# Graph network on one core: adjacency cast by GpSimd's loads, one bf16 copy of its rows read for two heads, operand halves made beside the first masks, flag read inside the last loop, output in four pieces

## What is computed

```python
# layer 0: attention over the neighbours, 4 heads of 64
ht = (h @ Wm).reshape(n, 4, 64); el = ht.al; er = ht.ar
scores = leaky_relu(el[:, :, None] + er.T[None], 0.2), -inf where adj == 0
out = softmax(scores) @ ht
# layer 1: GRU cell on (adj without diagonal) @ h; attention with 3 heads of 256,
# whose weights depend on the column alone; a second GRU cell on the mean of the heads
att = softmax(where(adj > 0, e[None, :], NEG_INF)); support += (att * adj) @ (h @ W)
# layer 2: concat(h, adj @ h / (deg + 1)) @ W.T
# layer 3: adds a term only where an adjacency value lies strictly between 0 and 1
```

## Time and profile before

| | |
|---|---|
| median of 3 runs | 1352.21 us |
| the profiled execution | 1358.34 us |
| its span | 1356.5 us, mean granted clock 0.929 |
| PE busy | 1152.5 us, 85% |
| DVE busy | 974.1 us, 72% |
| ACT busy | 808.2 us, 60% |
| POOL busy | 322.9 us, 24% |
| moved by DMA | 225.10 MB |
| a half row (704 KB), issue to landing, median | 5.3 us |

### The profile page before, as it was taken

The page is one execution under the profiler, slowest core; times in us unless marked ns, Lnnn a source line. Parts: engine busy times, 40 slices in busy tenths (PEclk is TensorE's granted clock), DMA queues, the critical chain, the costliest instruction groups (busy, mean ns, idle before and its releaser), DMA issues.

```text
span 1356.5 us, 35957 instructions
## 1 busy us (share of the span) xinstructions
PE 1152.5 (85%) x15055; PEld 944.2 (70%) x15055; DVE 974.1 (72%) x2219; ACT 808.2 (60%) x1232; POOL 322.9 (24%) x383
## 2 busy tenths in 40 slices
PE   4519888999867999899867999999899997778996
PEld 3419888999856776566635888887788654436885
DVE  5599897899983576676776999897995364552541
ACT  3468898999752233322326999897889365653000
POOL 4762323133041032333232111111120142220000
PEclk9859999999875999989987999999899998899998
DMA  9733445111026667677779778677752010020532
GB/s 320 241 135 121 176 131 186 35 35 66 3 71 214 198 222 253 211 246 254 272 257 345 228 273 323 220 249 250 263 191 102 5 32 13 18 92 1 192 108 84
DMA packets 89450, 225.10 MB, mean 166 GB/s; under 512 B 7506, under 2 KB 52674, under 8 KB 89026
## 3 DMA queue, kind: packets, MB, share of 16 engines
q1 hardware_dynamic: 88097, 222.21, 48.5%
q10 hardware_dynamic: 1184, 0.53, 0.1%
HBM read 202.98 MB, written 19.73 MB: 164 GB/s over the span
## 4 chain that ended last, share of the span: by engine, by line
PE 49%; DVE 16%; DMA 15%; issue 6%; ACT 6%; POOL 5%; SPq 1%; DVEq 0%; ACTq 0%; POOLq 0%
PE PS L1676 12%; DMA arena<-in_adj 12%; PE PS L1817 10%; PE PS L1818 10%; PE PS L1871 8%; DVE scratch L1372 3%; PE PS L1767 3%; DVE arena L1214 2%; PE PS L1858 2%; DVE arena L1220 2%; DVE arena L1160 2%; PE PS L1774 1%; PE PS L1711 1%; POOL X L738 1%; ACT arena L823 1%
## 5 line engine op out<-in xcount | busy, mean ns | idle before, releaser
L1817 PE MATMUL PS<-arena 128*128 128x257 f16 x1452 | 331.6, 276 | 21.5 <-ACT arena L968 14.9
L1818 PE MATMUL PS<-arena 128*128 128x257 f16 x1452 | 331.4, 277 | 0.0
L1676 PE MATMUL PS<-arena 128*128 128x65 f16 x7744 | 260.9, 196 | 72.3 <-DVE arena L1220 56.9
L1676 PEld LDWEIGHTS PS<-arena 128*128 128x128 fp8e4 x7744 | 257.3, 99 | 75.8 <-issue 59.9
L1372 DVE CUSTOM_DVE_ANT_0 scratch<-arena 128x1408 bf16<-128x1408 f32 x132 | 216.4, 1639 | 78.7 <-DMA arena<-in_adj 46.1
L865 ACT ACTIVATE arena<-arena 128x1024 fp8e4<-128x1024 f32 (+1 forms) x231 | 227.6, 1079 | 21.1 <-DVE arena L1214 20.7
L968 ACT ACTIVATE arena<-arena 128x896 int16<-128x896 uint8 (+1 forms) x198 | 187.3, 971 | 31.9 <-DVE arena L1425 22.4
L1817 PEld LDWEIGHTS PS<-arena 128*128 128x128 bf16 x1452 | 144.3, 99 | 47.5 <-ACT arena L968 13.2
L1818 PEld LDWEIGHTS PS<-arena 128*128 128x128 bf16 x1452 | 141.6, 97 | 23.1
L959 ACT ACTIVATE arena<-arena,E1B 128x896 uint8<-128x896 f32 (+1 forms) x131 | 139.1, 1062 | 13.1 <-DMA arena<-m_rows 13.1
L1214 DVE TENSOR_TENSOR arena<-arena,AT 128x256 int32<-128x256 int32 (+1 forms) x264 | 115.4, 437 | 26.7 <-ACT arena L865 23.8
(11 more groups left out here) (187 smaller groups left out, 1537.6 us busy)
## 6 DMA issues: line engine op xcount, KB each, us to landing
arena<-in_adj SPq DMA_DIRECT2D x176, 704.0 KB, 5.3
arena<-in_adjT SPq DMA_DIRECT2D x44, 512.0 KB, 7.6
hw_saved<-arena SPq DMA_DIRECT2D x22, 387.0 KB, 7.3
arena<-in_adjT SPq DMA_DIRECT2D x22, 384.0 KB, 5.1
arena<-hw_saved SPq DMA_DIRECT2D x9, 774.0 KB, 7.8
arena<-h_saved SPq DMA_DIRECT2D x44, 128.0 KB, 2.1
arena<-e_rows SPq DMA_DIRECT2D x3, 1408.0 KB, 7.3
arena<-el_rows SPq DMA_DIRECT2D x8, 512.0 KB, 5.4
```

The source lines that it names most:

```text
L1676: ins = pe.matmul(PS[:, k, q * C0:(q + 1) * C0], MASK[:, (m + j) % NMASK, q, k * P:(k + 1) * P], MOV[:, j, 2 * h + q, a, :], start=(j == 0 ...
L1817: pe.matmul(PS[:, k, 0:D + 1], weights, w[:, 0:D + 1], start=(j == 0), stop=False)
L1818: ins = pe.matmul(PS[:, k, 0:D + 1], weights, w[:, D + 2:2 * D + 3], start=False, stop=(j == NT - 1))
```

## The change

1. `STG`, `load_chunk`, `casts_at` and POOL's 66 casts go. POOL issues DMAs that read fp32 and write fp8 straight into `AT`: 22 of 128x768 (group A) ahead of all six splits, and 22 of 128x2048 (B and C) when all of `MOV` is there. The first mask of a group waits for all 22 transfers. SP does not load blocks any more; its first task after x is the six weight pieces.
2. Behind them POOL issues 22 DMAs from HBM to HBM that make a bf16 copy of the adjacency's rows (`AH_D`). Diagonal blocks, loaded by SP as fp32, are cleared by one POOL operation (128x2816) and written over the copy by 22 small DMAs. SP waits for all 44 before its loads of the edge weights.
3. The maxima read the bf16 copy, in a ring of two buffers. Each half row is loaded once for heads 0 and 1 (`EB` now holds both heads' scores): 88 maxima in steps 0 to 19 of the GRU stage, and 44 for head 2 in the attention, from step 8 on, one every 2.25 steps. `clear_diagonal` goes. The maxima of heads 0 and 1 are turned, saved and loaded together; those of head 2 are turned at step 19 of unit 4 and step 0 of unit 5.
4. The `MOV` loop is cut up: DVE does `weighted(m + 2)` and `low_part(m)` ahead of the masks of step m of unit 0, ACT `weighted_high(j + 2)` ahead of its threshold.
5. The flag is made after block 20 of the last loop, and the output is written in four pieces (8, 7, 5 and 2 blocks) and the remainder.

```diff
@@ the preamble @@
-            for n in range(4):
-                load_chunk(n)
             for i in range(4):
                 load_piece(RAW[:, i, :], pieces[i], f"raw{i}")
...
+            for i in range(len(pieces)):
+                sp.wait_ge(sem("ws"), i + 1)
+                save_piece(HALF[:, i % 4, :, :], pieces[i], f"ws_out{i % 4}")
+                if i + 4 < len(pieces):
+                    load_piece(RAW[:, i % 4, :], pieces[i + 4], f"raw{i % 4}")
             sp.wait_ge(sem("el_t"), 1)
             sp.dma_start(EL_D.rearrange("t h q -> (t h) q"), ELT[0:NT * H0, :]).then_inc(sem("el_rows"), 16)
             sp.wait_ge(sem("el_rows"), 16)
             load_el(0)
             load_el(1)
...
-            sp.wait_ge(sem("stg_used"), len(chunk0) - NT)
+            sp.wait_ge(sem("rows_h"), 16 * 2 * NT)
@@ POOL @@
             for t in range(NT):
-                pool.wait_ge(sem(f"stg{t % 4}"), 16 * (t // 4 + 1))
-                pool.tensor_copy(AT[:, t, 0:GA[0][1] * P], STG[:, t % 4, 0:GA[0][1] * P], saturate=False
-                                 ).then_inc(sem("stg_cast"), 1)
...
+                pool.dma_start(AT[:, t, 0:GA[0][1] * P], adjT[t, :, 0:GA[0][1] * P]).then_inc(sem("adj_a"), 16)
+            for i in range(len(pieces)):
+                pool.wait_ge(sem(f"raw{i % 4}"), 16 * (i // 4 + 1))
...
+                split(RAW[:, i % 4, :], HALF[:, i % 4, :, :], pieces[i][3], 3 * D)
...
             pool.wait_ge(sem("mov"), NT)
...
+            for t in range(NT):
+                pool.dma_start(AT[:, t, GA[0][1] * P:NT * P], adjT[t, :, GA[0][1] * P:NT * P]).then_inc(sem("adj_b"), 16)
+            for t in range(NT):
+                pool.dma_start(AH_D[t], t_in["adj"][t * P:(t + 1) * P, :]).then_inc(sem("rows_h"), 16)
+            pool.wait_ge(sem("dblk"), 16 * NT)
+            link(pool.tensor_tensor(DBLK, DBLK, NOTI[:].unsqueeze(1).to_broadcast([P, NT, P]), ALU.mult))
+            pool.wait_ge(sem("rows_h"), 16 * NT)
+            for t in range(NT):
+                pool.dma_start(AH_D[t, :, t * P:(t + 1) * P], DBLK[:, t, :]).then_inc(sem("rows_h"), 16)
@@ DVE, masks of layer 0 @@
-                if h == 0:
-                    dve.wait_ge(sem("stg_cast" if g == 0 else "stg_used"), j + 1 + (g - 1) * NT if g else j + 1)
+                if h == 0 and j == 0:
+                    dve.wait_ge(sem("adj_a" if g == 0 else "adj_b"), 16 * NT)
...
+            weighted(0)
+            weighted(1)
             for m in range(last + 1):
                 n, j = divmod(m, NT)
+                if m + 2 < NT:
+                    weighted(m + 2)
+                if m < NT:
+                    low_part(m)
                 positive_mask(m)
@@ maxima @@
+        PAIRED = 2 * 2 * NT
+            return min(PAIRED, -(-PAIRED * t // ROWS_LAST))
+        row_at = {8 + 9 * i // 4: 2 * NT + i for i in range(2 * NT)}
...
             def load_row(L):
...
+                if L >= 2:
+                    sp.wait_ge(sem("rmax"), maxima_after(L - 2))
+                sp.dma_start(AROW[:, L % 2, :], AH_D[t, :, c * QUARTER:(c + 1) * QUARTER]
+                             ).then_inc(sem(f"arow{L % 2}"), 16)
...
-            load_scores(EB, 0)
+            load_scores(EB[:, 0, :], 0)
+            load_scores(EB[:, 1, :], 1)
...
-                if (n, j) == (1, 18):
-                    maxima_turned(1, PS[0:NT, 7, 0:P])
-                if (n, j) == (5, 13):
-                    maxima_turned(2, PS[0:NT, 7, 0:P])
+                if (n, j) == (5, 0):
+                    maxima_turned(2, 1, 7)
@@ the end @@
+    OUT = [(0, 8), (8, 7), (15, 5), (20, 2)]
+                if t == CHECK_L2 + 2:
+                    dve.wait_ge(sem("sens_gmax"), 1)
+                    dve.tensor_scalar(sens_any[:], small[:, 21:22], 0.0, None, ALU.is_gt).then_inc(sem("flag"), 1)
...
-            dve.wait_ge(sem("sens_gmax"), 1)
-            dve.tensor_scalar(sens_any[:], small[:, 21:22], 0.0, None, ALU.is_gt).then_inc(sem("flag"), 1)
```

More of the change, by code:

```diff
@@ L172, in gnn_stack_kernel @@
         rows_at = a1.at
[L173 to L174 removed]
+        EB = a1.take(2, N)
+        AROW = a1.take(2, QUARTER, dt=BF16, size=2)
         rows_end = a1.at
+        CROW = arena[:, rows_at + N:rows_end].rearrange("p (a b) -> p a b", a=3)
         NSH = a1.take(2, DC, 2, 2 * P, dt=F16, size=2)
@@ L295, in gnn_stack_kernel @@
         banks_before.append(cnt)
-        stg_before = [16 * len(range(q, len(chunk0), 4)) for q in range(4)]
+        stg_before = [0] * 4
         def threshold_on_act(n, j):
@@ L516, in _ @@
                     load_halves(GWS, 0, "we")
-            for L in range(3):
+            for L in range(2):
                 load_row(L)
@@ L545, in load_maxima @@
                 b0, nb = G0[g]
-                sp.wait_ge(sem("mn"), 16 * (h + 1))
+                sp.wait_ge(sem("mn"), 16 if h < 2 else 32)
                 if n >= 2:
-                    for e in range(3):
+                    for e in range(2):
                         sp.wait_ge(sem(first_sem[e]), first_count[e][(n - 1) * NT])
@@ L576, in _ @@
                         load_products(0, c)
-            for L in range(ROWS_EDGE, ROWS_EDGE + 3):
+            for L in range(2 * NT, 2 * NT + 2):
                 load_row(L)
@@ L753, in _ @@
                     delta(t, 0, HR, GT)
-                    for L in range(rows_before(t + 1), rows_before(t + 2)):
-                        clear_diagonal(L)
                 if t >= 1:
@@ L851, in _, with weighted_high @@
             act.wait_ge(sem("coef"), 1)
-            for t in range(NT):
+            def weighted_high(t):
                 act.wait_ge(sem("t_b"), t + 1)
@@ L1161, in low_part, with weighted @@
                                   MOV[:, t, :, 0, :], ALU.subtract).then_inc(sem("mov"), 1)
-            for t in range(NT):
+            def weighted(t):
                 if t >= 3:
```

215 lines of the change are left out of this document (78 added, 137 removed).

## The result

The changed kernel takes **1374.99 us**, the median of four runs (1367.59 to 1378.57), against 1352.08 for the kernel before on the same chip (1351.28 to 1353.33): a ratio of 1.0139, 95% interval 1.0105 to 1.0172. It is 1.4% slower; the forecast was 30 us faster, and the range ended at 1358. The profiled execution took 1367.59 us with a span of 1364.1, so it is the fastest of the four, 7.4 under their median, while the one of before stood 6.1 above its own.

What follows compares the result with a forecast made beforehand. No engine was taken to bound the whole kernel; limits differed by stage. Gains of 2 + 15 + 10 + 3.5 = 30.5 us turned the median of 1352.2 into 1321.7, say 1322, with a range of 1304 to 1358.

Steps and rivals of the forecast that it cites:

- The gate at unit 4: Layer 0: unit 4 waits for the B and C loads until 182.6 against 181.65, 1 us lost.
- the cover: Layer 0: slack between the row copy's finish, 347 at most, and SP's need of it before 390; priced at nothing.
- The rival of slow casting transfers: Layer 0: casting loads at half rate, 170 GB/s, delay unit 4 by 68 us, total 1390; chance 0.17.
- The start: Up to unit 0's end: first mask at 70.5, steps of 1.91 us, end at 113.5; 3 us gained.
- the dear-issue rival: Start: each POOL issue takes 1.64 us, unit 0 and the gate come 14 us later, total 1336; chance 0.12.
- port: Start: POOL's issues wait for DVE's copies, 9 us later in all, total 1331; chance 0.05.
- The GRU stage: GRU stage: steps of 11.3 us with 4.4 maxima each, half-row loads mostly hidden; 15 us gained.
- the rival of 12.1: GRU stage: DVE binds it at 12.1 us per step or more, PE waiting in each, total 1337; chance 0.13.
- The attention: Attention: 5 us back at its start, 8 at head 2's turn, 3 off for the copy at unit 5; 10 gained.
- The end: Kernel's end: flag after block 20, last output issued by 1347.3 against 1350.7; 3.5 us gained.
- that rival: Kernel's end: the flag is no earlier because POOL's reduction takes long, total 1326; chance 0.05.

Runs made afterwards that it cites:

- e1: Changed kernel with all 22 row copies held back until the masks of unit 7 begin: 1361.47 us, 1.0038 of the kernel before.
- e6: Changed kernel without the DRAM row copy; POOL casts half rows into their buffer where needed and clears diagonals there: 1364.92 us, 1.0042 of the kernel before.
- e9: e6 plus an uncast copy that nobody reads, 22 transfers on SP's queue, one per 7 mask steps from unit 4: 1387.22 us, 1.0227 of the kernel before.
- e4: Changed kernel with ACT, in unit 0, making threshold j before the high part of j+2: 1361.24 us, 1.0042 of the kernel before.
- e8: Kernel before with only the change's end (flag inside the last loop, output in four pieces): 1350.80 us, 0.9950 of the kernel before.
- e5: e2 with each of the 22 row copies cut into four transfers: 1352.65 us, 0.9953 of the kernel before.
- e2: Changed kernel with row copies spaced one per 7 masks from unit 4, `DBLK` clearing ahead of them: 1357.36 us, 1.0012 of the kernel before.
- e11: e10 with ACT's threshold order of e4 in unit 0: 1334.42 us, 0.9859 of the kernel before.
- e10: e6 with a block's last diagonal clearings put behind POOL's subtraction for the GRU: 1350.53 us, 0.9966 of the kernel before.
- e3: e2 with loads of groups B and C spaced too, a gate for each, copies one per 5 masks from unit 5: 1359.49 us, 1.0012 of the kernel before.

## Why the prediction was wrong, point by point

**The step that failed** is in "The gate at unit 4": "The copy of the rows queues behind B and C ... All of this at nothing; if the cover went, it would cost what it is late beyond 390." I priced the copy by its own due time alone. It met that easily, landing at 250.8, sooner than my 275 to 322, and cost about 50 us all the same: 47.6 MB issued in 11.5 us kept the DMA engines full (share 1.03 from 120 to 250 us) while two others used them, SP's loads of row scores and the queue "instruction", which I read as the one that brings PE's program. Nothing on the critical path waited for the copy, but ACT waited 52.9 us for row scores beside it and the group loads. e1 (the wait moves with the copy), e6 (without the copy the waits are gone, and the gaps from unit 4 on) and e9 (an idle copy brings those gaps back) show it. The front of the argument had the row for it: the loads of row scores at 6.2 us are in the prediction as a constant, and nothing asked what they would be behind a full queue.

**The gate** itself was right. B and C were issued from 109.8 on, landed by about 174, the slowest taking 53.2 us: 23.1 MB in some 64 us, about 360 GB/s read, where I had 340 from the earlier trace rows. The copy was faster still: its packets, the 15.9 MB that it writes, ran from 170.7 to 249.9, and the 31.7 MB that it reads in that time are 400 GB/s, so it was done sooner than by either of my counts. Unit 4's thresholds began at 184.68, I had said 182.6. But they waited for row scores, not for B and C. The rival of slow casting transfers is refuted, though it named the right side and nearly the right size, 1390.

**The start.** I said 3 us for unit 0, it was 0.7. POOL's issue is 0.54 us (I took 1.0, the dear-issue rival 1.64), so everything began 10.6 us sooner; the step was 2.49 and not 1.91, which took it back. The two errors cancelled; that the term came out near is luck. I had summed DVE's work per step and not followed the loop ACT, DVE, ACT; e4 shows the 11.7 us in it. The 0.05 beside "port" in the chances were for issues of POOL that wait for DVE's copies, one copy of 0.41 us for each of the 22 issues of group A, 9 us later in all (1331). No run shows a port that the two share, and the issues did not wait for the copies: between 16.0 and 28.1 us, in which POOL issued group A, DVE was busy for 9.4 us and began six of its copies of 0.41 us, and behind the first issue (0.87 us) each of the next 20 took 0.52 or 0.53.

**The GRU stage**, 13.6 against 15, looks right, and in part by luck. The step was: 17 steps from 520.45 to 716.30 give 11.5 us, forecast 11.3, and the rival of 12.1 is refuted. Head 1's scores held the first low halves as described (4.70 us at 512.91, forecast 3). bf16 itself gave DVE nothing here: a maximum takes 1692 ns in the mean (L1344; 1630 in e6) against 1639 on fp32 (L1372 before). The rows are there in time and the diagonals are clear: DVE's idle time before its maxima in the stage fell from 69.7 to 15.8 us. But the stage now holds 88 maxima and not 73, DVE is busy there for 226.7 us and not 195.4, and little of the gain reached PE. Its waits for DVE's low halves, before and after:

```profile
PE PS L1734 <- DVE arena L1357: 25.0, 11, 5.4
PE PS L1706 <- DVE arena L1326: 20.9, 8, 4.9
```

The rest is mostly 4 us less of waiting for ACT at the attention's first matmul (8.41 before, 4.17 now) and some 6 less of PE's busy time for the same matmuls, 243.6 us against 249.7, at a granted clock of 0.98 against 0.95. e8, whose stage is the old one, took 276.3. How much of the 13.6 is the change's own is therefore open.

**The attention** gained 15.5 against 10, where I had looked for it: its first 30 us hold 235 matmuls where they held 173, which is 7 us, and the stretches of 20 us around unit 6 hold 169 or more, where one held 104. The 3 us that I took off for the copy at unit 5 did not show.

**The end**: 4.7 against 3.5, the fourth group's issue hidden entirely; e8 shows it alone. The flag was early, and that rival is refuted. The other 4 us of the last stretch lie in the second GRU, where PE spent 97.1 us on the same 396 matmuls (L1739, L1830) that had taken 100.9 (L1767, L1858). No change touches them; the granted clock was 0.97 in the 196 us behind the attention there, and 0.94 before. So these 4 us are not the change's.

**What stays open.** It is not known why four runs of the changed kernel spread over 11 us, and so why the medians differ by 22.9 where the profiled pair differs by 9.3; no trace of a slower execution was taken. Nor is it known why the packets of the queue "instruction" should start late: the traces show only that PE's gaps end behind them, and e5 that packets of 1,408 in place of 22,528 bytes left 15.0 of 19.2 us. Whether smaller packets would cure the long wait behind the unpaced copy was not tried.

## What to carry to other kernels

Price a bulk transfer by what shares the DMA engines with it while it runs, not by when it is due: look for small broadcast loads on the critical path and for gaps named "issue" in PE's timeline. Pacing removed the long waits here (52.9 us before it, 0.38 in e2) but not the gaps (10.1 us, and 19.2 in e2, between 190 and 300). What worked is fewer bytes in the stage that PE and ACT fill: the rows cast where they are used, in stages whose DMA share was 0.56 (e6, 430 to 700 us) and 0.60 (e11, 690 to 1047). That alone gave 1.0042 (e6); with POOL's subtraction put first (e10) and ACT's threshold put first (e11) it turned 1.4% slower into 1.4% faster. And when two engines pass a block back and forth, follow the loop through each engine's program order before taking the busier engine's work as the step.

## What the runs showed of the hardware that I had not expected

- Changed kernel, 120 to 250 us, DMA share 1.03: the loads of row scores of 512 KB on SP's queue landed after 34.0, 75.1 and 44.8 us, where the kernel before had 6.2 in the median. From 176 to 249 us 1543 packets of 512 bytes of SP's queue passed beside 662 packets of 22,528 bytes of the copy, 2.3 for each.
- Changed kernel, 100 to 400 us: PE had 16 gaps named "issue" of 0.7 us or more; of the 15 distances between them 13 are 127 or 128 matmuls and one is 256. In all fourteen traces such a gap ended 1.2 to 1.6 us after a packet of 16,384 bytes of the queue "instruction" had landed (164 of 164). "issue" and DMA share between 190 and 300 us:

| run | "issue", us | DMA share |
|---|---|---|
| e6, no copy | 1.1 | 0.11 |
| before | 6.6 | 0.26 |
| changed | 10.1 | 0.65 |
| e9, uncast copy on SP's queue | 13.5 | 0.44 |
| e5, casting copy, paced, in four | 15.0 | 0.62 |
| e2, casting copy, paced | 19.2 | 0.51 |
| e3, group loads paced too | 20.6 | 0.67 |

- A DMA issued by POOL took 11.97 / 22 = 0.54 us for group A. The casting transfers of B and C read 23.1 MB in some 64 us, 360 GB/s, where the plain fp32 loads before had 341 to 354. The page lists 256.0 KB for such a transfer, what it writes in fp8, a quarter of what it reads in fp32, and so has 116 GB/s between 120 and 160 us at a share of 1.06.
- POOL's clearing of 128x2816 took 6.64 us in the changed kernel; I had estimated 6 from an operation of 128x768.
